# Half stage of a graph kernel: one of two tiles weighed by GpSimd, both one-hot tiles made by VectorE

## The chip, the cores and the metric

One Trainium2 chip, one core of it. Times are device microseconds of one execution of the whole program, and the number compared is the median of several executions. A core has TensorE (PE in the profile, with PEld for its weight loads), VectorE (DVE), ScalarE (ACT), GpSimd (POOL) and SyncE (SP), each with an instruction stream of its own, tied together by semaphores.

## The reference: what is computed

A graph network of two layers with residuals and layer norms, on 6250 nodes with 64 features and 206,250 directed edges. This case is about the first layer, an attention layer with 4 heads of 64 features:

```python
out_i = softplus(concat([x[i], edge_attr]) @ W).reshape(-1, 4, 64)
out_j = softplus(concat([x[j], edge_attr]) @ W).reshape(-1, 4, 64)
alpha = softplus((concat([out_i, out_j], -1) * att).sum(-1))
# batch norm over the edges, softplus, softmax over the edges of node i
out   = segment_sum(out_j * alpha[:, :, None], i).mean(1) + bias
```

The inner sum over 128 features (64 of out_i and 64 of out_j, times att, for each of the 4 heads) is what the change moves between engines. A second layer, two graph convolutions, follows.

## The kernel before, in words

Edges are sorted into tiles of 128, one edge to a partition, so that all edges of a tile have their node i in one block of 128 nodes. Two tiles make a unit (UT = 2), six units a round (BU = 6). Earlier stages (`key_stage`, `table_stage`, `spread_stage`) write to memory, for each edge, a row with softplus(out_j) (256 numbers), the edge's 64 features and its node's place in the block. `half_stage` (L1464) computes the other half, out_i, and the sum with att. It has 912 units in 152 rounds; loops hold two rounds each (`paired_parts`), so a loop's end comes once in twelve units. `before(i, j, depth, width)` names the unit that lies `depth` back, `seg` the unit that lies ahead.

Each engine has its order written out by hand. For unit j:

- SP loads the unit's rows into one of six buffers `bufh` (L1516), as soon as the sums of the unit six before have been taken (`sp_read`).
- `places` on DVE makes the one-hot tile of the unit's first tile (L1546), three units ahead. POOL makes that of the second tile (L1528), keeps the places in `nloA` (L1530) and copies the 64 edge features of both tiles to `eaC` (L1534), as soon as the rows are in.
- `turn` on PE transposes the two one-hot tiles (L1623) and eaC (L1626), one unit ahead, in front of `product`: edge features times W (L1634) and one-hot tile times the node table in three parts (L1639), all into `pre`. `body` on PE calls `turn` of unit j+1 and then `product` of unit j.
- ACT copies what was turned to `eaTh` and `oneT` (L1587, L1588) two units ahead, and for the next unit takes Exp of `pre` (L1595) and Ln of that plus one (L1599) into the second half of `bufh`. The semaphore of that Ln is `sp_ready`.
- `finish` on DVE waits for `sp_ready`, and takes for each of the two tiles and each of the four heads one multiply-and-sum over 2 x 64 elements, `bufh` times `attb` (L1559: eight instructions, two SBUF inputs each, with one small read of the accumulator behind each). Once a round the sums are copied to `alpha` (L1572).

Other stages that the text draws on: `spread_stage` before it (DVE reduces 128x400 at L933), and `message_stage` after it (L2144), where POOL multiplies the units 1 and 4 of each round by their weights (L2203, 128x512), DVE the other four (L2248, the same shape) and adds PE's result, which lies in PSUM, to `acc` (L2257).

Of the kernel before, what the change touches and what calls it, by code (L numbers as in the profile page):

```python
# [15 lines left out]
fp32 = mybir.dt.float32  # L16
bf16 = mybir.dt.bfloat16
# [5 lines left out]
P = 128  # L23
D = 64
# [1439 lines left out]
def half_stage(nc, z, m, sb, ps, sem, att):  # L1464
# [3 lines left out]
    with ExitStack() as ctx:  # L1468
# [7 lines left out]
        attb = sb(ctx, "attb", [P, 2, H, D], fp32)  # L1476
        junk = [sb(ctx, f"junk{q}", [P, UT * H, 2, D], bf16) for q in range(2)]
        sums = sb(ctx, "sums", [P, BU * UT * H], fp32)
# [5 lines left out]
        def sems(name, n=BU):  # L1484
            return [sem(ctx, f"{name}{j}") for j in range(n)]

        row_in, ea_kept, one_ready, second_ready, x_turned, o_turned, x_evac, o_evac, pre_ready, exp_done, sp_ready, \
            sp_read = (sems(s) for s in (
                "row_in", "ea_kept", "one_ready", "second_ready", "x_turned", "o_turned", "x_evac", "o_evac",
                "pre_ready", "exp_done", "sp_ready", "sp_read"))  # L1490
# [29 lines left out]
        @block.gpsimd  # L1520
        def _(eng):
            def body(i, h):
                for j in range(BU):
                    o, c = before(i, j, PRE, BU)
                    eng.wait_ge(row_in[j], (i + 1) * 16)
                    wait(eng, o_turned[o], c)
                    eng.sem_inc(keeping, 1)
                    eng.tensor_scalar(one[j % PRE][:, 1, :], m["io128b"][:, :], buf[j][:, 1, 0, C + D:C + D + 1], 0.0,  # L1528
                                      ALU.add, ALU.is_equal).then_inc(second_ready[j], 1)
                    eng.tensor_copy(m["nloA"][:, span((i * BU + j) * UT, UT)], buf[j][:, :, 0, C + D])  # L1530
                    o, c = before(i, j, 2, BU)
                    wait(eng, x_turned[o], c)
                    eng.sem_inc(keeping, 1)
                    eng.tensor_copy(eaC[j % 2][:, :, :], buf[j][:, :, 0, C:C + D]).then_inc(ea_kept[j], 1)  # L1534

            paired_parts(eng, z.its, body)

        @block.vector
        def _(eng):
            def places(i, j):  # L1540

                q = j % PRE
                o, c = before(i, j, PRE, BU)
                eng.wait_ge(row_in[j], (i + 1) * 16)
                wait(eng, o_turned[o], c)
                eng.tensor_scalar(one[q][:, 0, :], m["io128b"][:, :], buf[j][:, 0, 0, C + D:C + D + 1], 0.0,  # L1546
                                  ALU.add, ALU.is_equal).then_inc(one_ready[j], 1)

            def finish(i, j):
                q = j % 2  # L1550
                o, c = before(i, j, 2, BU)
                eng.wait_ge(sp_ready[j], i + 1)
                wait(eng, sp_read[o], c)
                if j == 0:
                    wait(eng, kept, i)
                for k in range(UT):
                    for h in range(H):
                        n = (j * UT + k) * H + h
                        ins = eng.tensor_tensor_reduce(junk[q][:, k * H + h, :, :],  # L1559
                                                       buf[j][:, k, :, h * D:(h + 1) * D],  # L1560
                                                       attb[:, :, h, :], 1.0, 0.0, ALU.mult, ALU.add,
                                                       sums[:, n:n + 1])
                ins.then_inc(sp_read[j], 1)

# [50 lines left out]
        def _(eng):  # L1615
            def turn(i, j):
                q = j % 2
                o, c = before(i, j, 2, BU)
                eng.wait_ge(one_ready[j], i + 1)
                eng.wait_ge(second_ready[j], i + 1)  # L1620
                wait(eng, o_evac[o], c)
# [1048 lines left out]
```

## Time and profile before

| | |
|---|---|
| time, median of 3 executions | 7230.75 us (7227.9 to 7233.67) |
| span of the profiled execution, first to last instruction | 6311.7 us |
| profiled execution's own total | not given; the median lies 919 us above the span |
| busy over the span: PE, DVE, ACT, POOL | 76%, 78%, 62%, 63% |
| half stage | 2526 to 4470 us |

Times in the rows are microseconds from the start of the span, unless marked ns. Register, branch, semaphore and DMA-issuing instructions don't count as busy. In a timeline a row is start, duration, engine, line, operation, output <- input, shape, count, and in brackets the idle time of the engine before it with what ended it. DVE's and ACT's instructions overlap a little, so what one costs its engine is the distance of two starts. The multiply-and-sum is called CUSTOM_DVE_ANT_1 in the profile. A span on POOL is rough.

### The profile page before, as it was taken

To read this page: it belongs to the slowest core of one execution; us is meant where nothing else is said; L and a number is where in the kernel's file an instruction comes from. 1 tells how busy PE (TensorE), PEld (TensorE's weight loads), DVE (VectorE), ACT (ScalarE), POOL (GpSimd) and SP (SyncE) were. 2 spreads that over 40 slices of the span, in tenths; PEclk is the share of its full clock that TensorE was granted. 3 is DMA by queue.
4 is the path that set the end of the run, shared out by engine and by line. 5 is a ranking of instruction groups with operands and counts; after the bars stand their busy time and mean duration, and the time that the engine had idled before them with its cause. 6 is when DMAs were issued, how large, how long until landed. Compare 5 with 4: busy or idle time off the path is not lost. (4 is left out here: it accounts for less than half of the span.)

```text
span 6311.7 us, 164797 instructions
## 1 busy us (share of the span) xinstructions
PE 4769.4 (76%) x33037; PEld 3113.2 (49%) x33038; DVE 4917.3 (78%) x25722; ACT 3904.0 (62%) x10209; POOL 3956.6 (63%) x5713
## 2 busy tenths in 40 slices
PE   1367777777777773888888888888388888875976
PEld 0234444444444442444444444444155555555976
DVE  6579888888888882999999999999777777774122
ACT  3057666666666663788888888888666666660000
POOL 1357777777777775666666666666299998870000
PEclk8589999999999997999999999999699999996978
DMA  8856666666666665555555555555277777764766
GB/s 236 261 193 228 224 222 222 213 225 222 223 213 223 222 224 198 157 155 155 155 156 155 156 155 156 155 155 155 54 219 221 221 222 218 217 190 184 317 276 234
DMA packets 905821, 1259.83 MB, mean 200 GB/s; under 512 B 267668, under 2 KB 774531, under 8 KB 884180
## 3 DMA queue, kind: packets, MB, share of 16 engines
q1 hardware_dynamic: 783812, 843.53, 47.3%
q0 software_dynamic: 88656, 333.99, 13.8%
q10 hardware_dynamic: 33216, 80.75, 3.5%
q8 instruction: 54, 0.88, 0.1%
q14 instruction: 83, 0.68, 0.0%
HBM read 832.07 MB, written 425.87 MB: 199 GB/s over the span
## 5 line engine op out<-in xcount | busy, mean ns | idle before, releaser
L872 POOL DMA_INDIRECT rows<-rowS,idx x1616 | 1628.5, 1008 | 521.3 <-issue 485.5
L1559 DVE CUSTOM_DVE_ANT_1 junk<-bufh,attb 128x128 bf16<-128x128 f32 x7296 | 1738.1, 298 | 7.0 <-ACT bufh L1599 5.5
L1528 POOL TENSOR_SCALAR one<-io128b,bufh 128x128 bf16<-128x128 bf16 x912 | 811.1, 889 | 723.1 <-DMA bufh<-rows 723.0
L2282 PE MATMUL psm<-msg,onem 128*128 128x260 f32 x3648 | 926.9, 396 | 177.7 <-issue 157.5
L1128 PE MATMUL psa<-one_c,one_s 128*128 128x392 bf16 x2352 | 560.2, 350 | 483.4 <-ACT cnts L1014 442.0
L2282 PEld LDWEIGHTS psm<-msg,onem 128*128 128x128 f32 x3648 | 644.3, 190 | 459.9 <-issue 388.9
L955 DVE TENSOR_SCALAR one_c<-ioc,code 128x392 bf16<-128x392 f16 x2352 | 790.4, 336 | 13.8
L1639 PE MATMUL pre<-P3h,oneT 128*128 x5472 | 756.5, 274 | 0.0
L1595 ACT ACTIVATE lg<-pre 128x512 f32<-128x512 f32 x912 | 544.6, 597 | 309.1 <-PE pre L1639 303.4
L2248 DVE TENSOR_TENSOR msg<-oj,alpha 128x512 f32<-128x512 f32 x608 | 494.0, 813 | 220.2 <-issue 196.2
L2218 ACT ACTIVATE dist_m<-io,nloA 128x128 f32<-128x128 f32 x1216 | 454.9, 398 | 335.3 <-PE psm L2282 325.3
L1634 PE MATMUL pre<-W2d,eaTh 64*128 64x256 f32 x3648 | 641.6, 429 | 0.0
L1639 PEld LDWEIGHTS pre<-P3h,oneT 128*128 128x128 bf16 x5472 | 460.5, 98 | 344.7 <-issue 302.4
L2207 POOL TENSOR_SCALAR onem<-io,lanes 128x128 f32<-128x128 f32 x608 | 601.7, 993 | 29.3 <-POOL heads L2194 29.3
L1021 ACT ACTIVATE lgS<-preS 128x1024 f32<-128x1024 f32 x404 | 412.5, 1021 | 329.1 <-PE preS L1117 323.6
L956 DVE TENSOR_SCALAR one_s<-io128b,pairS 128x128 bf16<-128x128 bf16 x2352 | 595.4, 253 | 0.0
L1599 ACT ACTIVATE bufh<-lg 128x512 f32<-128x512 f32 x912 | 575.9, 632 | 29.0
L1559 DVE DVE_READ_ACCUMULATOR2_ANT sums<- 128x1 f32 x7296 | 559.0, 77 | 0.1
L1111 PE MATMUL preS<-W2d,eaT 64*128 64x256 f32 x3232 | 528.4, 451 | 3.1 <-ACT eaT L1032 2.9
L1128 PEld LDWEIGHTS psa<-one_c,one_s 128*128 128x128 bf16 x2352 | 202.1, 101 | 653.0 <-issue 340.5
L1623 PE MATMUL turned<-identb,one 128*128 128x128 bf16 x1824 | 256.9, 222 | 264.2 <-DVE one L1546 170.7
L1014 ACT ACTIVATE cnts<-psa 128x392 bf16<-128x392 f32 x784 | 361.1, 486 | 137.3 <-PE psa L1128 134.9
(275 smaller groups left out, 8757.5 us busy)
## 6 DMA issues: line engine op xcount, KB each, us to landing
bufh<-rows SPq DMA_DIRECT2D x912, 322.0 KB, 3.0
oj<-rows SPq DMA_DIRECT2D x912, 256.0 KB, 2.9
adj<-adj SPq DMA_DIRECT2D x98, 1568.0 KB, 8.2
adj<-cnts ACTq DMA_DIRECT2D x49, 1568.0 KB
eaS<-in_edge_attr_dram SPq DMA_DIRECT2D x201, 256.0 KB
low<-dlow SPq DMA_DIRECT2D x202, 252.0 KB
rows<-blanktail POOLq DMA_DIRECT2D x20, 1610.0 KB
rows<-fill POOLq DMA_DIRECT2D x100, 322.0 KB
```

The costliest lines, as they stand in the source:

```text
L872: eng.indirect_dma_start(out=m["rows"][h], out_offset=bass.IndirectOffsetOnAxis(ap=idx[s][:, k:k + 1], axis=0), in_=rows[s][:, k, :], in_o ...
L955: eng.tensor_scalar(one_c[r][:, k, :], m["ioc"][:, :], code[r][:, k:k + 1], None, ALU.is_equal)
L956: ins = eng.tensor_scalar(one_s[r][:, k, :], m["io128b"][:, :], pair[q][:, k, 0:1], 0.0, ALU.add, ALU.is_equal)
L1128: mm = eng.matmul(psa[r][:, 0:z.GC], one_s[r][:, k, :], one_c[r][:, k, :], start=(k == 0), stop=(k == GT - 1))
L1528: eng.tensor_scalar(one[j % PRE][:, 1, :], m["io128b"][:, :], buf[j][:, 1, 0, C + D:C + D + 1], 0.0, ALU.add, ALU.is_equal).then_inc(secon ...
L1559: ins = eng.tensor_tensor_reduce(junk[q][:, k * H + h, :, :], buf[j][:, k, :, h * D:(h + 1) * D], attb[:, :, h, :], 1.0, 0.0, ALU.mult, AL ...
L1595: eng.activation(lg[q][:, :, :], pre[q][:, :, 0:C], ACT.Exp, accum_out=m["exps"][:, span(2 * z.NG + i * BU + j, 1)]).then_inc(exp_done[j], 1)
L1599: eng.activation(buf[j][:, :, 1, 0:C], lg[q][:, :, :], ACT.Ln, bias=1.0).then_inc(sp_ready[j], 1)
L1634: eng.matmul(pre[j % PRE][:, k, 0:C], eaT[q][k * D:(k + 1) * D, :], m["W2d"][k * D:(k + 1) * D, :], start=True, stop=False, skip_group_che ...
L1639: mm = eng.matmul(pre[j % PRE][:, k, 0:C], oneT[q][:, k * P:(k + 1) * P], P3[:, bass.ds(b, 1), n, :].rearrange("p o c -> p (o c)"), start= ...
L2207: eng.tensor_scalar(one[j][:, 1, :], m["io128"][:, :], lanes[:, j * UT + 1:j * UT + 2], 0.0, ALU.add, ALU.is_equal).then_inc(second_ready[ ...
L2282: mm = eng.matmul(psm[j][:, 0:C + H], one[q][:, k, :], msg[q][:, k, :], start=(k == 0), stop=(k == UT - 1))
```

## The change

POOL no longer makes the second one-hot tile; DVE makes both, in `places`. POOL multiplies the second tile of each unit (both halves, 512 numbers) by att into a new tile `prod`, of which there are two, when the unit's Ln is there; DVE keeps the four multiply-and-sums of the first tile and sums `prod` by one reduction. On POOL the copies are made two units ahead of the product. PE has one wait less.

```diff
-        junk = [sb(ctx, f"junk{q}", [P, UT * H, 2, D], bf16) for q in range(2)]
+        junk = [sb(ctx, f"junk{q}", [P, H, 2, D], bf16) for q in range(2)]
+        prod = [sb(ctx, f"prodh{q}", [P, 2, H, D], fp32) for q in range(2)]
...
         @block.gpsimd
         def _(eng):
+            def keep(i, j):
+                eng.wait_ge(row_in[j], (i + 1) * 16)
+                eng.sem_inc(keeping, 1)
+                eng.tensor_copy(m["nloA"][:, span((i * BU + j) * UT, UT)], buf[j][:, :, 0, C + D])
+                o, c = before(i, j, 2, BU)
+                wait(eng, x_turned[o], c)
+                eng.sem_inc(keeping, 1)
+                eng.tensor_copy(eaC[j % 2][:, :, :], buf[j][:, :, 0, C:C + D]).then_inc(ea_kept[j], 1)
+
+            def weigh(i, j):
+                o, c = before(i, j, 2, BU)
+                eng.wait_ge(sp_ready[j], i + 1)
+                wait(eng, sp_read[o], c)
+                eng.sem_inc(keeping, 1)
+                eng.tensor_tensor(prod[j % 2][:, :, :, :], buf[j][:, 1, :, 0:C].rearrange("p s (h d) -> p s h d", h=H),
+                                  attb[:, :, :, :], ALU.mult).then_inc(weighed[j], 1)
+
             def body(i, h):
                 for j in range(BU):
-                    o, c = before(i, j, PRE, BU)
-                    eng.wait_ge(row_in[j], (i + 1) * 16)
-                    wait(eng, o_turned[o], c)
-                    eng.sem_inc(keeping, 1)
-                    eng.tensor_scalar(one[j % PRE][:, 1, :], m["io128b"][:, :], buf[j][:, 1, 0, C + D:C + D + 1], 0.0,
-                                      ALU.add, ALU.is_equal).then_inc(second_ready[j], 1)
-                    eng.tensor_copy(m["nloA"][:, span((i * BU + j) * UT, UT)], buf[j][:, :, 0, C + D])
-                    o, c = before(i, j, 2, BU)
-                    wait(eng, x_turned[o], c)
-                    eng.sem_inc(keeping, 1)
-                    eng.tensor_copy(eaC[j % 2][:, :, :], buf[j][:, :, 0, C:C + D]).then_inc(ea_kept[j], 1)
-
+                    if not (last(i) and j + 2 >= BU):
+                        keep(*seg(i, j + 2, BU))
+                    weigh(i, j)
+
+            eng.wait_ge(att_in, 32)
+            keep(0, 0)
+            keep(0, 1)
             paired_parts(eng, z.its, body)
...
-                eng.tensor_scalar(one[q][:, 0, :], m["io128b"][:, :], buf[j][:, 0, 0, C + D:C + D + 1], 0.0,
-                                  ALU.add, ALU.is_equal).then_inc(one_ready[j], 1)
+                for k in range(UT):
+                    ins = eng.tensor_scalar(one[q][:, k, :], m["io128b"][:, :], buf[j][:, k, 0, C + D:C + D + 1], 0.0,
+                                            ALU.add, ALU.is_equal)
+                ins.then_inc(one_ready[j], 1)
...
-                for k in range(UT):
-                    for h in range(H):
-                        n = (j * UT + k) * H + h
-                        ins = eng.tensor_tensor_reduce(junk[q][:, k * H + h, :, :],
-                                                       buf[j][:, k, :, h * D:(h + 1) * D],
-                                                       attb[:, :, h, :], 1.0, 0.0, ALU.mult, ALU.add,
-                                                       sums[:, n:n + 1])
-                ins.then_inc(sp_read[j], 1)
+                n = j * UT * H
+                for h in range(H):
+                    eng.tensor_tensor_reduce(junk[q][:, h, :, :], buf[j][:, 0, :, h * D:(h + 1) * D],
+                                             attb[:, :, h, :], 1.0, 0.0, ALU.mult, ALU.add, sums[:, n + h:n + h + 1])
+                eng.wait_ge(weighed[j], i + 1)
+                eng.tensor_reduce(sums[:, n + H:n + 2 * H], prod[q][:, :, :, :].rearrange("p s h d -> p h s d"), AX.XY,
+                                  ALU.add).then_inc(sp_read[j], 1)
...
                 eng.wait_ge(one_ready[j], i + 1)
-                eng.wait_ge(second_ready[j], i + 1)
                 wait(eng, o_evac[o], c)
```

## Rows read from the trace of the kernel before

**Rows 1.** Busy time by stretch: a part of the spread stage, the half stage.

```profile
600.00:1000.00 400.00, 305.33 (x2319) 191.00 (x2318) 342.98 (x1541) 267.60 (x458) 307.34 (x305) 0.92 0.65 219
...
2526.00:4470.00 1944.00, 1696.60 (x11856) 961.27 (x11856) 1887.01 (x15656) 1598.93 (x4560) 1252.54 (x2736) 1.00 0.58 155
```

Columns: stretch, its length, busy time and count of PE, PEld, DVE, ACT, POOL, granted clock, DMA's share, GB/s.

**Rows 2.** Groups of instructions, whole span: busy us, mean ns, idle before.

```profile
L1559 DVE CUSTOM_DVE_ANT_1 junk<-bufh,attb 128x128 bf16<-128x128 f32 x7296 | 1738.1, 298 | 7.0 <-ACT bufh L1599 5.5
L1528 POOL TENSOR_SCALAR one<-io128b,bufh 128x128 bf16<-128x128 bf16 x912 | 811.1, 889 | 723.1 <-DMA bufh<-rows 723.0
```

**Rows 3.** Timeline of DVE in the half stage, from 3202.9 us.

```profile
3202.91 0.32 DVE L1546 TENSOR_SCALAR one<-io128b,bufh 128x128 bf16<-128x128 bf16 x1
3203.07 0.28 DVE L1559 CUSTOM_DVE_ANT_1 junk<-bufh,attb 128x128 bf16<-128x128 f32 x1
...
3203.28 0.28 DVE L1559 CUSTOM_DVE_ANT_1 junk<-bufh,attb 128x128 bf16<-128x128 f32 x1
...
3203.49 0.36 DVE L1559 CUSTOM_DVE_ANT_1 junk<-bufh,attb 128x128 bf16<-128x128 f32 x1
```

**Rows 4.** Waits from 3000 to 3500 us: in total, times, longest.

```profile
POOL one L1528 <- DMA bufh<-rows: 176.9, 235, 1.7
PEld turned L1623 <- DVE one L1546: 94.4, 181, 1.3
```

**Rows 5.** Groups of instructions on DVE: the reduction in the spread stage.

```profile
L933 DVE TENSOR_REDUCE posf<-ranks 128x8 f32<-128x400 f32 x202 | 112.8, 558 | 0.2
```

**Rows 6.** Timeline of DVE at a loop's end, from 3196.2 us.

```profile
3196.29 0.24 DVE L1572 COPY alpha<-sums 128x48 f32 x1
3196.88 0.25 DVE L1546 TENSOR_SCALAR one<-io128b,bufh 128x128 bf16<-128x128 bf16 x1 [0.35 <-issue]
```

**Rows 7.** Timeline of POOL and DVE in the message stage, 4909 to 4912.5 us.

```profile
4909.08 1.06 POOL L2203 TENSOR_TENSOR msg<-oj,heads 128x512 f32<-128x512 f32 x1
4909.43 1.25 DVE L2248 TENSOR_TENSOR msg<-oj,alpha 128x512 f32<-128x512 f32 x1 [0.51 <-issue]
4910.11 2.09 POOL L2207 TENSOR_SCALAR onem<-io,lanes 128x128 f32<-128x128 f32 x2
...
4910.95 0.68 DVE L2248 TENSOR_TENSOR msg<-oj,alpha 128x512 f32<-128x512 f32 x1
...
4912.17 0.43 DVE L2257 TENSOR_TENSOR acc<-acc,psm 128x260 f32 x1 [0.21 <-PE psm L2282]
4912.23 1.06 POOL L2203 TENSOR_TENSOR msg<-oj,heads 128x512 f32<-128x512 f32 x1
```

**Rows 8.** Timeline of POOL, PE and ACT in the half stage, 3203 to 3207 us.

```profile
3203.13 0.26 POOL L1530 COPY nloA<-bufh 128x2 f32 x1
...
3203.34 0.38 POOL L1534 COPY eaC<-bufh 128x128 f32<-128x128 f32 x1
...
3203.76 0.33 PE L1626 MATMUL turned<-ident,eaC 128*128 128x128 f32 x1 [0.19 <-POOL eaC L1534]
...
3204.66 0.83 PE L1639 MATMUL pre<-P3h,oneT 128*128 x6
...
3205.61 0.60 ACT L1595 ACTIVATE lg<-pre 128x512 f32<-128x512 f32 x1 [0.64 <-PE pre L1639]
...
3206.33 0.63 ACT L1599 ACTIVATE bufh<-lg 128x512 f32<-128x512 f32 x1
```

**Rows 9.** Timeline of POOL at the half stage's start.

```profile
2527.37 0.18 POOL L1530 COPY nloA<-bufh 128x2 f32<-128x2 f32 x1
2527.49 0.28 POOL L1534 COPY eaC<-bufh 128x128 f32<-128x128 f32 x1
```

**Rows 10.** Timeline of DVE and ACT: one unit's one-hot tile and the Ln behind it.

```profile
3200.96 0.24 DVE L1546 TENSOR_SCALAR one<-io128b,bufh 128x128 bf16<-128x128 bf16 x1
...
3203.91 0.63 ACT L1599 ACTIVATE bufh<-lg 128x512 f32<-128x512 f32 x1
```

**Rows 11.** DMA issues on the page: KB each, median us from issue to landing.

```profile
bufh<-rows SPq DMA_DIRECT2D x912, 322.0 KB, 3.0
```

More of the change, by code:

```diff
@@ L1485, in sems @@
             return [sem(ctx, f"{name}{j}") for j in range(n)]
-        row_in, ea_kept, one_ready, second_ready, x_turned, o_turned, x_evac, o_evac, pre_ready, exp_done, sp_ready, \
+        row_in, ea_kept, one_ready, weighed, x_turned, o_turned, x_evac, o_evac, pre_ready, exp_done, sp_ready, \
             sp_read = (sems(s) for s in (
-                "row_in", "ea_kept", "one_ready", "second_ready", "x_turned", "o_turned", "x_evac", "o_evac",
+                "row_in", "ea_kept", "one_ready", "weighed", "x_turned", "o_turned", "x_evac", "o_evac",
                 "pre_ready", "exp_done", "sp_ready", "sp_read"))
```

## The prediction, made before the changed kernel was built or run

> **What bounds the kernel now.** I read the busy time by stretch first. The half stage is the stretch from 2526 to 4470 us, 1944 us for 912 units of two tiles, so 2.13 us a unit; VectorE is busy for 1887 of them, PE for 1697, ScalarE for 1599, POOL for 1253, and PE's granted clock is 1.00, its upper level of 2.4 GHz [rows 1]. The groups of instructions tell what VectorE does: eight multiply-and-sum instructions of line 1559 a unit, one one-hot tile of line 1546, while POOL makes the other (line 1528) [rows 2, 3]. The timeline gives their true cost, which is the distance of two starts: 0.21 us from 3203.07 to 3203.28, and 0.16 us for a one-hot tile, 3202.91 to 3203.07 [rows 3]. The waits say that the others run behind VectorE or the row loads: in 500 us POOL waits 176.9 us for rows, PE's weight loads 94.4 us for VectorE's one-hot tile [rows 4]. Nothing holds VectorE up but its own queue. It is the bound of the stage, and a unit is 8 x 0.21 + 0.16, two instructions stretched by 0.08 each (3203.49 takes 0.36 where 3203.28 takes 0.28), and loop and copy costs.
>
> **The change, part by part, on VectorE.** Removed: four of eight multiply-and-sums, 4 x 0.21 = 0.85 us. Added: a second one-hot tile, 0.16 to 0.17, and one reduction of 512 fp32 elements to 4. The nearest row is a reduction of 400 elements in 0.558 us [rows 5]. Were all of that fixed, 512 would cost 0.56, were all of it per element, 0.558 x 512/400 = 0.71; I take 0.67, near the second, which is 0.60 start to start (instructions of 0.28 start 0.21 apart, so 0.07 overlap [rows 3]). An upper bound is 1.2, if the permuted view halved the rate; the ring below would cover that too, as VectorE has some 0.5 us to spare in it. VectorE's own work per unit becomes 0.33 + 0.85 + 0.60 + 0.04 (the copy of the sums, 0.24 once in six [rows 6]) = 1.82, and with two stretches of 0.08 by POOL's copies 1.98 us. Against 2.13 that alone would be a gain of 0.13 us a unit after loop costs.
>
> **On POOL.** Removed: its one-hot tile, 0.889 us [rows 2]. Added: a product of 512 fp32 elements with two inputs. The same shape runs on POOL in the message stage: 1.06 us, 1.03 to the next start, 4909.08 to 4910.11 [rows 7]. There one input is a broadcast, here it is a plain tile; I take 1.03, between 0.95 and 1.2. POOL's busy time, some 1.6 us a unit, is no bound. Two things about the product are.
>
> **First: the ring that it closes.** The new order on POOL is keep(0), keep(1), and then keep(j+2), weigh(j) for each unit. keep makes eaC, from which PE's line 1626 turns the tile; weigh(j) waits for sp_ready(j), ScalarE's Ln. Before, POOL waited for nothing that late. Now keep(j+1) stands behind weigh(j-2) in POOL's queue; PE turns unit j+1 ahead of the product of unit j (lines 1644 to 1649: turn, then product), so product(j) waits for keep(j+1); Exp and Ln of j follow, and weigh(j) waits for that Ln. This is a ring that goes round once in two units: weigh(j-2), keep(j+1), turn(j+1), product(j), Exp(j), Ln(j), weigh(j). Its price, from one pass of the profile [rows 8]: keep, from the start of the copy nloA at 3203.13 to the end of eaC at 3203.34 + 0.38 = 3203.72: 0.59. From there to the end of Ln, 3206.33 + 0.63 = 3206.96: 3.24 (turn at 3203.76, P3 products 3204.66 to 3205.49, Exp at 3205.61). Ln's end to POOL's start: 0.05, as from eaC's end to PE's turn in the same rows, 0.04. The product: 1.03. Sum 4.91 us in two units, **2.46 us a unit**. With keep as it runs undisturbed, 0.12 + 0.28 = 0.40 [rows 9], the sum is 4.72, or 2.36; with a product of 1.2 it is 5.1, or 2.55. I take 2.46, since POOL's copies stand beside VectorE's two-input work as they do now. Every part of the ring is a duration that a row shows, and the order is written out in the code; so the ring is the step of which I am surest.
>
> **Second: the port.** The message stage shows what POOL's product does to VectorE. VectorE's product of line 2248 takes 0.68 us alone, at 4910.95; the one that starts at 4909.43, inside POOL's product of 4909.08 to 4910.14, takes 1.25. It ended at 4910.68, so in effect it began 0.68 earlier, at 4910.00, 0.14 us before POOL's ended. VectorE's add of line 2257, which reads PSUM as one of its inputs, takes 0.43 from 4912.17 with POOL's product beside it from 4912.23: not held [rows 7]. So a VectorE instruction with two SBUF inputs stands still for the first 0.90 us of a POOL product of 1.06. The multiply-and-sums have two SBUF inputs; the one-hot tile is stretched in the half stage by POOL's work too, 0.32 at 3202.91 where 3200.96 took 0.24 [rows 3, 10], so I count it as held. The reduction has one input and nothing in PSUM; I take it as free, from the add.
>
> The Trainium skill, in SBUF — State Buffer, section SBUF: two separate sides, has this as a lock on a shared pair of ports, held "for the full instruction". For the product the trace nearly agrees (0.90 of 1.06). For POOL's copies it doesn't: eaC takes 0.38 us and costs the multiply-and-sum beside it 0.08 [rows 3, 8]. By the rule the held work would add up to 0.33 + 0.85 + 1.06 + 0.26 + 0.38 = 2.88 us a unit, by the row to 0.33 + 0.85 + 0.90 + 0.17 = 2.25, which is below the ring.
>
> Where does the 0.90 fall? If POOL's product(j+1) starts while VectorE reduces unit j, then part of it hides behind the reduction. Take a pitch of 2.46 and time 0 at the end of POOL's product(j): VectorE is freed at -0.15, makes its one-hot tiles until 0.2, the four sums until about 1.15, reduces until 1.8. POOL's next product starts at 2.46 - 1.06 = 1.40, inside the reduction, and holds VectorE until 2.31. So VectorE stands 0.5 us, its unit is 1.98 + 0.5 = 2.48, and it doesn't wait for weighed at all. That agrees with the ring, and its one-hot tiles are early enough: from their end to Ln's end are 3.34 us (3201.20 to 3204.54 [rows 10]), so the product of two units later may start at 0.2 + 3.4 = 3.6, and the ring asks it for 3.86. Both fit.
>
> **Edits at nothing.** PE's dropped wait is one of two for the same tile. The tiles of prod are used by turns, and POOL's wait for sp_read two units back is over (reduction ends at 1.8, product(j+2) starts at 3.86). Row loads are freed at the reduction's end, and three units, 7.4 us, lie before keep needs the row; the load takes 3.0 [rows 11]. POOL's new wait for att is in front of rows that land later on the same queue. Loop ends cost 0.35 us once in twelve units [rows 6], 0.03 a unit.
>
> **Sum.** 912 x (2.46 + 0.03) = 2271, and 10 for filling and draining (before: 7 to the first sum): 2281 against 1944, +337 us. The other stages are untouched. The profiled execution has a span of 6311.7; its own total isn't shown, and the median of the runs lies 919 above the span. I add the difference to the median: 7230.75 + 337 = **7568 us**. The ring's bounds, 2.36 and 2.55, give 7477 and 7650.
>
> **Rivals.**
> - *Product over the sums.* If POOL's product comes while VectorE still does its multiply-and-sums, nothing hides it: 1.98 + 0.90 + 0.03 = 2.91 us a unit, 2654 + 10, +720: 7951 us. It sustains itself: one-hot tiles end, 3.40 later POOL's product starts, and at a pitch of 2.88 that is 0.52 into the next unit's four sums, of which the last starts at 0.64. For it: at the start VectorE's sums and POOL's product of a unit wait for the same Ln. Against: the margin is 0.12 us, and once it slips past the last sum the shorter pitch holds. By the full rule of the page the pitch would be 2.88 too. Chance 0.22; with turns between both, times between 7568 and 7951, 0.13.
> - *The clock falls.* PE gets more gaps. In the spread stage, with PE busy for 305 of 400 us, the granted clock is 0.92, which is 16% of the time at 1.2 GHz [rows 1]; in the half stage it would be busy for 1.86 of 2.46 us, the same share. PE's part of the ring is 1.73 us; a sixth of it again is 0.28 in two units, 0.14 x 912 = +128: 7696 us. Against: the clock is 1.00 now, with PE idle for an eighth of the stage. Chance 0.10.
> - *Faster.* POOL's product doesn't set the pace, VectorE does: 2.01 x 912 + 10 = 1843, -101: 7130 us. It needs a ring under 4.02 us, or 4.2 to break even, so a POOL product under some 0.3 us, or a ring that is not closed, and a port that doesn't hold the sums. The rows speak against each. Chance 0.04. That the new instructions don't appear as written, with no measurable difference: 0.02.
> - The ring as forecast: 0.49.
>
> **Numbers.** Predicted 7568. The range takes the ring's low bound, the clock, and the uncovered product: 7470 to 7955, leaving out under 0.2. The runs of before spread by 0.08%, so 0.2%, 14 us, is about the least that can be told from nothing. Faster by more: 0.05; within: 0.02; slower: 0.93.
>
> **What would show it.** Right: in the half stage VectorE's sums or one-hot tiles of over 1 us once a unit, beginning inside a POOL product; PE's line 1626 waiting for POOL's eaC in nearly every unit; eaC beginning right behind a POOL product; 2.4 to 2.6 us from one POOL product to the next. A reduction near 0.67. The first rival shows POOL's product starting between two sums and a pitch of 2.9. Wrong: PE waiting for one-hot tiles and not for eaC, VectorE busy with short instructions for over nine tenths, or a POOL product far from 1.06.

## The result, and the profile after

| | median | runs | lowest to highest |
|---|---|---|---|
| before | 7230.67 us | 4 | 7227.9 to 7233.67 |
| after | 7598.36 us | 4 | 7580.75 to 7606.47 |

The ratio is 1.0508, with a 95% interval of 1.0493 to 1.0523: 367.7 us slower, where 337 were forecast. One thing has to be cleared first. The profile shown of before has a span of 6311.7 us, 919 less than its runs, and that of after 7578.9, 2 less than its run. The kernel before was therefore profiled again (run before_again below). The missing time lies in the spread stage, whose code the change leaves alone: 2094 us in the first profile, 3014 in the second and in that of after. It goes with the chip: the kernel before takes 7227 us on the one on which keep3, early and keep3_early ran, and 6315 or 6317 on the two others. All comparisons below are with runs of the kernel before on the same chip, and differences are what carries over; the half stage itself is the same in both, 1943 and 1950 us.

The busy time by stretch, of the changed kernel's half stage and of 500 us in its middle; the columns are those of [rows 1]:

```profile
3426.00:5733.00 2307.00, 1695.57 (x11856) 960.67 (x11856) 2280.82 (x10183) 1652.02 (x4560) 1421.30 (x2736) 1.00 0.48 130
4300.00:4800.00 500.00, 368.81 (x2584) 208.96 (x2585) 495.69 (x2221) 359.61 (x995) 308.36 (x595) 1.00 0.49 131
```

2307 us for 912 units are 2.53 a unit, against 2.13 [rows 1]; the stage grew by 357 us against before_again and by 364 against the first profile, of 368. VectorE is "busy" in 496 of 500 us, with 36 fewer instructions per round than before. PE's granted clock stays at 1.00.

The groups of instructions of the same kernel, from the page (busy us, mean ns, idle before), answer to [rows 2] and [rows 5]:

```profile
L1537 POOL TENSOR_TENSOR prodh<-bufh,attb 128x512 f32<-128x512 f32 x912 | 1087.8, 1193 | 882.9 <-ACT bufh L1613 882.9
...
L1573 DVE CUSTOM_DVE_ANT_1 junk<-bufh,attb 128x128 bf16<-128x128 f32 x3648 | 916.0, 302 | 3.5 <-ACT bufh L1613 3.5
...
L1560 DVE TENSOR_SCALAR one<-io128b,bufh 128x128 bf16<-128x128 bf16 x1824 | 809.9, 484 | 59.2 <-DMA bufh<-rows 59.2
...
L1576 DVE TENSOR_REDUCE sums<-prodh 128x4 f32<-128x512 f32 x912 | 615.8, 675 | 0.0
```

The reduction came out at 0.675 us, as forecast. POOL's product takes 1.18 to 1.19 instead of 1.06. The line to look at is the one-hot tile's: a mean of 484 ns, where the median of the same line is 249 and the longest 1221. That is not work but standing. One more line stands, the copy of the sums to `alpha`, once in six units:

```profile
L1586 DVE COPY alpha<-sums x152: 201/984/990, 3447.0 to 5733.5; 128x48 f32 x142, 128x48 f32<-128x48 f32 x10
```

(Shortest, median and longest in ns.) Its median is 984 ns, where it took 0.24 us in [rows 6]. The timeline shows both, of VectorE, POOL, PE and ScalarE together, from one product of POOL to the next but one:

```profile
4402.39 1.18 POOL L1537 TENSOR_TENSOR prodh<-bufh,attb 128x512 f32<-128x512 f32 x1 [1.28 <-ACT bufh L1613]
...
4402.64 0.98 DVE L1586 COPY alpha<-sums 128x48 f32 x1
...
4403.54 0.44 DVE L1560 TENSOR_SCALAR one<-io128b,bufh 128x128 bf16<-128x128 bf16 x2
4403.63 0.31 POOL L1530 COPY eaC<-bufh 128x128 f32<-128x128 f32 x1
...
4404.04 0.29 PE L1636 MATMUL turned<-identb,one 128*128 128x128 bf16 x2 [1.16 <-DVE one L1560]
...
4405.01 0.83 PE L1652 MATMUL pre<-P3h,oneT 128*128 x6
...
4405.97 0.60 ACT L1609 ACTIVATE lg<-pre 128x512 f32<-128x512 f32 x1 [0.88 <-PE pre L1652]
...
4406.69 0.63 ACT L1613 ACTIVATE bufh<-lg 128x512 f32<-128x512 f32 x1
...
4407.52 1.17 POOL L1537 TENSOR_TENSOR prodh<-bufh,attb 128x512 f32<-128x512 f32 x1 [1.30 <-ACT bufh L1613]
4407.53 1.22 DVE L1560 TENSOR_SCALAR one<-io128b,bufh 128x128 bf16<-128x128 bf16 x1
```

From product to product but one are 5.13 us, two units. At 4407.53 a one-hot tile starts beside a product and takes 1.22 us; at 4402.64 it is the copy of the sums that starts beside one, and takes 0.98. And there is the first surprise: PE waits for one-hot tiles (line 1560), in this pass 1.16 us. The waits from 4300 to 4800 us say the same of 199 units; a wait for eaC isn't among them, though this view lists only waits of 0.15 us and more:

```profile
POOL prodh L1537 <- ACT bufh L1613: 190.4, 198, 1.4
PEld turned L1636 <- DVE one L1560: 186.7, 199, 1.4
PE turned L1636 <- DVE one L1560: 131.4, 199, 1.2
```

So two theories of the pitch stood at this point. **Queue**: keep(j+1) behind weigh(j-2) in POOL's queue closes the ring, as the prediction had it; eaC ends at 4403.94, 0.2 us before its turn, and at 4406.22 only 0.06 before, so it could well be the bound by a hair. **Port**: POOL's product holds VectorE's one-hot tiles, PE waits for these, and ring and hold are one thing. A unit without the copy of the sums shows how close the two are:

```profile
4404.65 1.21 POOL L1537 TENSOR_TENSOR prodh<-bufh,attb 128x512 f32<-128x512 f32 x1 [0.71 <-ACT bufh L1613]
...
4405.35 0.72 DVE L1560 TENSOR_SCALAR one<-io128b,bufh 128x128 bf16<-128x128 bf16 x2
...
4405.93 0.29 POOL L1530 COPY eaC<-bufh 128x128 f32<-128x128 f32 x1
...
4406.13 0.29 PE L1636 MATMUL turned<-identb,one 128*128 128x128 bf16 x2 [0.29 <-DVE one L1560]
4406.28 0.33 PE L1639 MATMUL turned<-ident,eaC 128*128 128x128 f32 x1
...
4408.86 0.63 ACT L1613 ACTIVATE bufh<-lg 128x512 f32<-128x512 f32 x1
...
4409.69 1.19 POOL L1537 TENSOR_TENSOR prodh<-bufh,attb 128x512 f32<-128x512 f32 x1 [0.63 <-ACT bufh L1613]
```

PE starts on the one-hot tiles 0.06 us after they are done (4406.07) and turns eaC 0.15 behind that, 0.06 after eaC is done (4406.22). Where eaC is early, the two starts lie 0.12 apart (4404.04 and 4404.16). So here eaC comes last, by 0.02 to 0.03 us, and that is so in five of six units of the trace; in the sixth, behind the copy of the sums, it is the one-hot tiles.

### The profile page after: what moved, and what is told of

It reads as the page before. It is cut to its first block and busy times, and to the rows that moved or that the text cites. A ratio compares the mean times of both kernels' runs of the same rounds, so it can differ in the third digit from the quotient of the medians.

```text
span 7578.9 us, 160271 instructions
## 1 busy us (share of the span) xinstructions
PE 5063.1 (67%) x33037; PEld 3242.9 (43%) x33038; DVE 5287.6 (70%) x20250; ACT 3967.1 (52%) x10209; POOL 4124.8 (54%) x5713
## 5 line engine op out<-in xcount | busy, mean ns | idle before, releaser
L1537 POOL TENSOR_TENSOR prodh<-bufh,attb 128x512 f32<-128x512 f32 x912 | 1087.8, 1193 | 882.9 <-ACT bufh L1613 882.9
L1128 PE MATMUL psa<-one_c,one_s 128*128 128x392 bf16 x2352 | 627.1, 387 | 838.6 <-DVE one_s L956 591.5
L1573 DVE CUSTOM_DVE_ANT_1 junk<-bufh,attb 128x128 bf16<-128x128 f32 x3648 | 916.0, 302 | 3.5 <-ACT bufh L1613 3.5
L1560 DVE TENSOR_SCALAR one<-io128b,bufh 128x128 bf16<-128x128 bf16 x1824 | 809.9, 484 | 59.2 <-DMA bufh<-rows 59.2
L1128 PEld LDWEIGHTS psa<-one_c,one_s 128*128 128x128 bf16 x2352 | 217.8, 109 | 1039.2 <-DVE one_s L956 652.4
L2220 POOL TENSOR_SCALAR onem<-io,lanes 128x128 f32<-128x128 f32 x608 | 617.1, 1022 | 29.3 <-POOL heads L2207 29.3
L1111 PE MATMUL preS<-W2d,eaT 64*128 64x256 f32 x3232 | 611.9, 504 | 12.3 <-issue 7.2
L1576 DVE TENSOR_REDUCE sums<-prodh 128x4 f32<-128x512 f32 x912 | 615.8, 675 | 0.0
L924 DVE TENSOR_TENSOR ranks<-psr,base 128x400 f32<-128x400 f32 x202 | 115.7, 573 | 692.0 <-remote 381.2
```

Source lines behind the costliest of these rows:

```text
L1111: eng.matmul(pre[h][:, q, a * C:(a + 1) * C], eaT[j][q * D:(q + 1) * D, 2 * h + a, :], m["W2d"][q * D:(q + 1) * D, :], start=(a == 0), sto ...
L1128: mm = eng.matmul(psa[r][:, 0:z.GC], one_s[r][:, k, :], one_c[r][:, k, :], start=(k == 0), stop=(k == GT - 1))
L1537: eng.tensor_tensor(prod[j % 2][:, :, :, :], buf[j][:, 1, :, 0:C].rearrange("p s (h d) -> p s h d", h=H), attb[:, :, :, :], ALU.mult).then ...
L1560: ins = eng.tensor_scalar(one[q][:, k, :], m["io128b"][:, :], buf[j][:, k, 0, C + D:C + D + 1], 0.0, ALU.add, ALU.is_equal)
L1573: eng.tensor_tensor_reduce(junk[q][:, h, :, :], buf[j][:, 0, :, h * D:(h + 1) * D], attb[:, :, h, :], 1.0, 0.0, ALU.mult, ALU.add, sums[:, ...
L1576: eng.tensor_reduce(sums[:, n + H:n + 2 * H], prod[q][:, :, :, :].rearrange("p s h d -> p h s d"), AX.XY, ALU.add).then_inc(sp_read[j], 1)
```

## The experiments

Pitches are the length of the half stage, from its first to its last instruction on `bufh` and `sums`, by 912.

| run | against before | half stage | us a unit |
|---|---|---|---|
| before (both profiles) | | 1943, 1950 us | 2.13, 2.14 |
| after | +367.7 | 2308 | 2.53 |
| keep3 | +356.5 | 2291 | 2.51 |
| early | +653.0 | 2593 | 2.84 |
| keep3_early | +614.3 | 2564 | 2.81 |
| aligned | +217.7 | 2158 | 2.37 |
| no_product | -196.7 | 1742 | 1.91 |
| free_product | +568.3 | 2510 | 2.75 |
| onehot_only | +73.0 | 2014 | 2.21 |
| extra_product | +729.5 | 2673 | 2.93 |
| psum_extra | +12.3 | 1969 | 2.16 |
| psum_before | -109.9 | 1835 | 2.01 |
| psum_keep3_early | +240.4 | 2181 | 2.39 |

**before_again.**

> The kernel before, unchanged, for a second profile. The profile shown of it has a span of 6311.7 us and its runs take 7230.7; the changed kernel's span is 2 us under its own time. Theory: the 919 us lie in the spread stage, which took 2094 us in the profile of before and 3014 in that of after, though the change doesn't touch it, and the runs of before had the long one too: span near 7229, half stage 1944 us (2.13 us a unit). Rival: the half stage of the timed runs is itself longer than 1944, and the change's price is less or more than the 363 us that the two profiles give.

Span 7218.6 us. The busy time by stretch, of its spread stage and its half stage:

```profile
356.00:3370.00 3014.00, 1901.10 (x12214) 1136.70 (x12214) 1763.39 (x7959) 1417.32 (x2395) 1600.19 (x1605) 0.79 0.46 154
3424.00:5374.00 1950.00, 1702.71 (x11856) 964.58 (x11856) 1887.95 (x15656) 1602.26 (x4560) 1254.73 (x2736) 1.00 0.57 154
```

The theory holds: the half stage is as in [rows 1], the spread stage 920 us longer with the same instructions. The cause is open.

**keep3.** POOL's copies come three units ahead:

```diff
-        eaC = [sb(ctx, f"eaC{q}", [P, UT, D], fp32) for q in range(2)]
+        eaC = [sb(ctx, f"eaC{q}", [P, UT, D], fp32) for q in range(PRE)]
...
-                    if not (last(i) and j + 2 >= BU):
-                        keep(*seg(i, j + 2, BU))
+                    if not (last(i) and j + PRE >= BU):
+                        keep(*seg(i, j + PRE, BU))
                     weigh(i, j)
```

> The changed kernel with POOL's copies three units ahead of the product instead of two (three eaC tiles). It opens the ring through POOL's queue: keep(j+1) then stands behind weigh(j-3). Queue theory (this ring sets the 2.53 us a unit of the changed kernel): the pitch falls, to 2.25 to 2.42, total 7390 to 7500. Port theory (the one-hot tiles, held by POOL's product, set it): nothing changes within 20 us, 7580 to 7615, and PE goes on waiting for line 1560's tiles.

7583.55 us against 7227.05, ratio 1.0486 (1.0465 to 1.0507). The queue theory in its own terms falls: its ring is open, and 2.53 became 2.51 where 2.25 to 2.42 had been expected. The intervals of the two ratios overlap, so even the 0.02 can't be told from nothing. The timeline of this kernel:

```profile
4402.99 1.18 POOL L1537 TENSOR_TENSOR prodh<-bufh,attb 128x512 f32<-128x512 f32 x1 [0.80 <-ACT bufh L1614]
...
4403.08 1.30 DVE L1561 TENSOR_SCALAR one<-io128b,bufh 128x128 bf16<-128x128 bf16 x2
...
4404.44 0.28 PE L1637 MATMUL turned<-identb,one 128*128 128x128 bf16 x2 [0.96 <-DVE one L1561]
...
4407.94 1.18 POOL L1537 TENSOR_TENSOR prodh<-bufh,attb 128x512 f32<-128x512 f32 x1 [0.80 <-ACT bufh L1614]
```

The ring goes by the other link: the product of 4402.99 holds the one-hot tiles of 4403.08 for a microsecond, they are done at 4404.38, PE takes them at 4404.44, and two units later POOL starts again, 4.95 us on. Both paths close a ring of nearly the same length, and this edit opens only one.

**early.** VectorE makes the one-hot tiles between the four sums and the reduction:

```diff
                     eng.tensor_tensor_reduce(...)
+                if not (last(i) and j + PRE + 1 >= BU):
+                    places(*seg(i, j + PRE + 1, BU))
                 eng.wait_ge(weighed[j], i + 1)
                 eng.tensor_reduce(...)
...
-                    if not (last(i) and j + PRE >= BU):
-                        places(*seg(i, j + PRE, BU))
                     finish(i, j)
```

> The changed kernel with the one-hot tiles of unit j+4 made on VectorE between the four sums and the reduction of unit j, instead of those behind the reduction: they then come before POOL's next product starts. Port theory (one-hot tiles held by the product are late for PE): the pitch falls to 2.40 to 2.47, total 7480 to 7540, if nothing stands behind it; queue theory: eaC is just as late, so the pitch stays at 2.50 to 2.53, total 7570 to 7610, and PE now waits for eaC instead of one-hot tiles. A rival on the other side: POOL's product now falls on the sums, 2.9 us a unit, 7930.

7880.0 us against 7227.05, ratio 1.0911 (1.0893 to 1.0929): the rival on the other side, and neither theory's first answer. The timeline of this kernel:

```profile
4403.33 0.28 DVE L1573 CUSTOM_DVE_ANT_1 junk<-bufh,attb 128x128 bf16<-128x128 f32 x1
4403.54 0.28 DVE L1573 CUSTOM_DVE_ANT_1 junk<-bufh,attb 128x128 bf16<-128x128 f32 x1
...
4403.59 1.27 POOL L1537 TENSOR_TENSOR prodh<-bufh,attb 128x512 f32<-128x512 f32 x1 [0.98 <-DVE sums L1578]
...
4403.75 1.26 DVE L1573 CUSTOM_DVE_ANT_1 junk<-bufh,attb 128x128 bf16<-128x128 f32 x1
4404.94 0.28 DVE L1573 CUSTOM_DVE_ANT_1 junk<-bufh,attb 128x128 bf16<-128x128 f32 x1
```

POOL now waits for line 1578, the reduction that frees its tile, so the product starts right behind a reduction, in every unit, and the third sum pays for it: 1.26 us. Nothing hides it. It is the first rival of the prediction, at 2.84 a unit where 2.91 was worked out. In the changed kernel the tiles and copies that come late for PE were what delayed POOL's product until the next reduction.

**keep3_early.** Both edits.

> Both edits: copies three units ahead and one-hot tiles before the reduction. If both rings are closed at the same length (queue and port), only this one is faster: VectorE's own 1.98 us and a hold of 1.03 (product 1.18 less 0.15) of which at most 0.6 hides behind the reduction, 2.4 us a unit, total 7480. If VectorE's occupancy alone sets the pace, nothing changes, 7580 to 7610. If the product comes earlier and meets the sums: 2.9 to 3.0 a unit, 7930 to 8030.

7841.39 us against 7227.05, ratio 1.0852 (1.0831 to 1.0873), the third case of the expectation, though 2.81 and +614 lie below its 2.9 to 3.0 and +700 to +800. POOL's product itself waits for only 71 us in all, but the copy in front of it in the queue waits for rows, now three units ahead: 841 us in the 2270 from 3430 to 5700.

```profile
4406.27 0.20 POOL L1526 COPY nloA<-bufh 128x2 f32 x1 [1.11 <-DMA bufh<-rows]
...
4406.76 1.18 POOL L1537 TENSOR_TENSOR prodh<-bufh,attb 128x512 f32<-128x512 f32 x1
```

So the row loads now set when the product starts, on the median 0.6 us after what it waits for itself is there. It then holds a sum in some seven of ten units and a one-hot tile in most of the others. Removing both rings makes the kernel slower: they had put more of the product beside the reduction (0.39 us a unit in the changed kernel, 0.16 here).

**no_product.** POOL's product is left out and VectorE reduces zeros, which are written once ahead of the loop.

```diff
-                    weigh(i, j)
+                    pass
...
-                eng.wait_ge(weighed[j], i + 1)
                 eng.tensor_reduce(...)
```

> The changed kernel without POOL's product: VectorE reduces tiles of zeros that are filled once, and doesn't wait for POOL; everything else is as in the changed kernel, so the weights of every second tile are left out. It takes away the hold and the ring at once and shows VectorE's own work. Both theories: 1.85 to 2.0 us a unit, half stage 1690 to 1840, total 6980 to 7130. Rival (the reduction or the second one-hot tile, not the product, costs more than counted): over 2.2 us a unit, over 7300.

6118.6 us against 6315.27 on its chip, ratio 0.9687 (0.967 to 0.9703): -196.7 us, where -100 to -250 had been expected (the absolute numbers stand for a chip with 7230). VectorE's own work is 1.91 us a unit with its loop costs. The product on POOL costs 2.53 - 1.91 = 0.62 us a unit, 565 us; the relief that it buys is 0.22. The traces tell on what the 0.62 falls. From this kernel to the changed one, the mean of a one-hot tile goes from 256 to 484 ns (0.46 us a unit), of a sum from 284 to 302 (0.07), and of the copy of the sums from 229 to 960, once in six units (0.12).

**free_product.** POOL's product waits for no Ln and multiplies att by itself:

```diff
-                eng.wait_ge(sp_ready[j], i + 1)
                 wait(eng, sp_read[o], c)
                 eng.sem_inc(keeping, 1)
-                eng.tensor_tensor(prod[j % 2][:, :, :, :], buf[j][:, 1, :, 0:C].rearrange("p s (h d) -> p s h d", h=H),
+                eng.tensor_tensor(prod[j % 2][:, :, :, :], attb[:, :, :, :],
                                   attb[:, :, :, :], ALU.mult).then_inc(weighed[j], 1)
```

> The changed kernel with a POOL product of the same size that multiplies att by itself and waits for no Ln, only for its tile to be read: the sums of every second tile are left out. No ring goes through it any more, the port is used as before. Port theory: the product now starts as soon as the reduction two units back has freed its tile, so it falls on the one-hot tiles and sums and nothing hides it: 1.98 + 1.03 = 3.0 us a unit, total 8030, slower than the changed kernel. Queue theory: without the ring VectorE's own pace, 2.0 to 2.4, total 7120 to 7480.

6883.6 us against 6315.27, ratio 1.0903 (1.0885 to 1.0921): +568.3, slower than the changed kernel's +367.7 although nothing waits for Ln on POOL. The direction is the port theory's; the size is 2.75 instead of 3.0, because this product takes 1.04 us and not 1.18 and VectorE's own work is 1.91 and not 1.98. The timeline:

```profile
3202.76 1.04 POOL L1536 TENSOR_TENSOR prodh<-attb 128x512 f32<-128x512 f32 x1 [1.15 <-DVE sums L1575]
...
3202.83 1.13 DVE L1572 CUSTOM_DVE_ANT_1 junk<-bufh,attb 128x128 bf16<-128x128 f32 x1
3203.89 0.28 DVE L1572 CUSTOM_DVE_ANT_1 junk<-bufh,attb 128x128 bf16<-128x128 f32 x1
```

The sum takes 0.85 us more than its 0.28, and 1.91 + 0.85 = 2.76 is the pitch.

**onehot_only.** The part of the change that moves the one-hot tile, alone, on the kernel before.

> The kernel before with one part of the change: VectorE makes both one-hot tiles, POOL only copies, and all eight sums stay on VectorE. Expected by every theory: one more one-hot tile, 0.16 to 0.17, less up to 0.08 for the POOL instruction that no longer stretches one of VectorE's: 2.21 to 2.30 us a unit, total 7305 to 7385. If it costs more than that, the hold isn't the main part of the change's price.

6388.29 us against 6315.27, ratio 1.0114 (1.0097 to 1.0131): +73.0 us, 0.08 a unit, at the low end (75 had been the least): a one-hot tile more on VectorE costs 0.16, and the POOL instruction that goes no longer stretches one of its sums.

**extra_product.** The kernel before, and one product more on POOL that nobody reads:

```diff
+                    o, c = before(i, j, 2, BU)
+                    wait(eng, weighed[o], c)
+                    eng.sem_inc(keeping, 1)
+                    eng.tensor_tensor(prod[j % 2][:, :, :, :], attb[:, :, :, :], attb[:, :, :, :],
+                                      ALU.mult).then_inc(weighed[j], 1)
```

> The kernel before, complete, with one more POOL product a unit of 512 elements (att by att) into a tile that nobody reads. It prices the hold on VectorE alone. POOL's own work becomes 0.89 + 0.18 + 0.30 + 1.18 = 2.5 us a unit. Port theory: VectorE, with eight sums and one one-hot tile and no reduction to hide behind, is held for 1.03 a unit: 2.13 + 1.03 = 3.1, total 8130. Rival (no hold on the multiply-and-sums, POOL itself becomes the bound): 2.5 to 2.6 us a unit, total 7570 to 7660.

7044.77 us against 6315.27, ratio 1.1156 (1.1138 to 1.1175): +729.5, 0.80 us a unit, for work whose result goes nowhere. 8130 had been expected on a chip with 7230, that is +900. The product here takes 1.07 us (median), and VectorE doesn't stand for all of it: the instruction that is held starts 0.11 us after the product, on the median, and is let go 0.13 before its end, which leaves 0.83.

**psum_extra.** The same kernel, with att copied once into a bank of PSUM, so that the sums have one input in SBUF (`pre` gets two tiles instead of three to make room, and PE's product waits accordingly):

```diff
-        pre = [ps(ctx, f"pre{q}", [P, UT, 2 * C], fp32) for q in range(PRE)]
+        pre = [ps(ctx, f"pre{q}", [P, UT, 2 * C], fp32) for q in range(2)]
+        attp = ps(ctx, "attp", [P, 2, C], fp32)
...
-                                                       attb[:, :, h, :], 1.0, 0.0, ALU.mult, ALU.add,
+                                                       attp[:, :, h * D:(h + 1) * D], 1.0, 0.0, ALU.mult, ALU.add,
...
+            eng.tensor_copy(attp[:, :, :], attb[:, :, :, :].rearrange("p s h d -> p s (h d)")).then_inc(att_kept, 1)
+            eng.wait_ge(att_kept, 1)
```

> The kernel with the extra POOL product (2.93 us a unit, 729 us over before), and att in PSUM. The direct test of the port: the same POOL product beside the same multiply-and-sums, which now have one SBUF input. Port theory: they are not held, only the one-hot tile is; POOL's own work of 2.4 to 2.5 us then sets the pitch, 2.4 to 2.65, half stage 2190 to 2420, 250 to 480 us over before; no multiply-and-sum over 0.5 us in the trace. Rival (the hold comes from something else, as SBUF banks or POOL's writes): 2.9 as before.

6328.83 us against 6316.57, ratio 1.0018 (1.0008 to 1.0028). +729.5 us became +12.3. This is the experiment that settles the matter for the sums. The groups of instructions, first of extra_product:

```profile
L1567 DVE CUSTOM_DVE_ANT_1 junk<-bufh,attb 128x128 bf16<-128x128 f32 x7296 | 2294.2, 374 | 5.0 <-ACT bufh L1607 4.8
```

and of psum_extra:

```profile
L1569 DVE CUSTOM_DVE_ANT_1 junk<-bufh,attp 128x128 bf16<-128x128 f32 x7296 | 1585.1, 279 | 38.3 <-ACT bufh L1611 19.2 <-issue 0.5
L1556 DVE TENSOR_SCALAR one<-io128b,bufh 128x128 bf16<-128x128 bf16 x912 | 369.6, 405 | 24.4 <-issue 22.1 <-DMA bufh<-rows 1.8
```

The same 7296 sums beside the same POOL products, 374 ns on the mean with att in SBUF and 279 with att in PSUM; the longest was 1.50 us and is 0.33. The one-hot tile (both its inputs in SBUF, one of them the scalar of the partition) is still held, 405 ns on the mean and 1.68 at most. That also answers a rival which this edit alone leaves, that the sums stood because both engines read the one tile of att: the one-hot tile and the copy of the sums (0.84 us at most here, 1.05 in extra_product) don't read it and are held beside the same product. POOL's pitch came out better than expected, 2.07 us in the timeline, as its own instructions no longer wait either: the one-hot tile on POOL takes 0.73 instead of 0.88.

**psum_before.** The kernel before with att in PSUM, and for that two tiles of `pre` instead of three.

> The kernel before, with att in a bank of PSUM instead of SBUF (pre has two buffers for three, to free it). The eight multiply-and-sums have one SBUF input each. Port theory: POOL's three instructions no longer stretch them, 2 x 0.08 a unit less: 1.97 to 2.05 us a unit if an input from PSUM costs VectorE nothing, 80 to 150 us under before. Rival: an input from PSUM costs each multiply-and-sum some fixed time, 8 x 0.03 or more: 100 us or more over before. Second rival: two buffers for pre stop PE: PE would wait for Exp, line 1595.

6206.72 us against 6316.57, ratio 0.9826 (0.981 to 0.9843): **faster than the kernel before**, by 110 us, with nothing left out. The timeline of VectorE:

```profile
3202.43 0.28 DVE L1561 CUSTOM_DVE_ANT_1 junk<-bufh,attp 128x128 bf16<-128x128 f32 x1
3202.64 0.28 DVE L1561 CUSTOM_DVE_ANT_1 junk<-bufh,attp 128x128 bf16<-128x128 f32 x1
3202.84 0.28 DVE L1561 CUSTOM_DVE_ANT_1 junk<-bufh,attp 128x128 bf16<-128x128 f32 x1
```

No sum of 0.36 is left [rows 3], and the longest of all is 0.291. An input from PSUM costs nothing: 0.21 us from start to start, as before. In the stage's 1835 us PE is busy for 1682 and ScalarE for 1597, VectorE for 1746; that little more is to be had on VectorE alone is an inference from this and wasn't tested.

**psum_keep3_early.** keep3_early with att in PSUM.

> The changed kernel with copies three units ahead, one-hot tiles before the reduction, and att in PSUM. Neither ring is left and the sums aren't held; the product starts at a reduction's end and runs beside the four sums. Port theory: what stays is VectorE's own 1.85 to 1.91 us and what of the hold reaches the one-hot tiles, 0.2 to 0.3: 2.05 to 2.2 us a unit, within 80 us of the kernel before on either side, and some 300 us faster than the changed kernel. Rival (the order, not the port, makes 2.81): stays above 2.6, over 430 us above before.

6556.95 us against 6316.57, ratio 1.0381 (1.0364 to 1.0399), +240.4 where 80 at most had been expected. The sums are free (longest 0.289), the pitch is 2.39 all the same. Its timeline shows two of the costs that the expectation had left out or made too small:

```profile
3201.62 0.42 DVE L1563 TENSOR_SCALAR one<-io128b,bufh 128x128 bf16<-128x128 bf16 x2 [0.66 <-DMA bufh<-rows]
...
3206.50 1.18 POOL L1539 TENSOR_TENSOR prodh<-bufh,attb 128x512 f32<-128x512 f32 x1
...
3206.65 1.24 DVE L1563 TENSOR_SCALAR one<-io128b,bufh 128x128 bf16<-128x128 bf16 x2
```

With one-hot tiles made four units ahead VectorE waits for row loads (159 us in the stage, 4 in no_product), and the tiles themselves are still held: their mean is 359 ns where it is 256 in no_product, 188 us. The third cost is the copy of the sums, 717 ns on the mean for 229, 74 us. Together that is 417 of the 439 us that this stage is longer than that of no_product.

**aligned.** keep3_early, with POOL's product of unit j+1 also waiting for the last sum of unit j:

```diff
                 wait(eng, sp_read[o], c)
+                o, c = before(i, j, 1, BU)
+                wait(eng, summed[o], c)
                 eng.sem_inc(keeping, 1)
                 eng.tensor_tensor(prod[...]
...
+                ins.then_inc(summed[j], 1)
```

> The kernel with copies three units ahead and one-hot tiles before the reduction (2.81 us a unit), and POOL's product of unit j+1 now also waits for the last sum of unit j. So it starts when VectorE has only two one-hot tiles and the reduction before its next sums. Port theory (the hold costs only what isn't hidden behind work with one input): part of the hold of 1.03 falls on the one-hot tiles, the rest hides behind the reduction, as does POOL's start: 1.91 + 1.03 - 0.45 = 2.45 to 2.6 us a unit, half stage 2230 to 2370, 290 to 430 us over the kernel before. Rival (the pitch of 2.81 has another cause, as PE's slower clock or the later one-hot tiles): it stays at 2.8 or grows, 600 us or more over before.

6534.25 us against 6316.57, ratio 1.0342 (1.0325 to 1.036), +217.7: a wait added takes keep3_early from 2.81 to 2.37 us a unit, below the range expected. The timeline:

```profile
3204.87 0.43 DVE L1564 TENSOR_SCALAR one<-io128b,bufh 128x128 bf16<-128x128 bf16 x2
3205.22 0.67 DVE L1583 TENSOR_REDUCE sums<-prodh 128x4 f32<-128x512 f32 x1
...
3205.22 1.18 POOL L1540 TENSOR_TENSOR prodh<-bufh,attb 128x512 f32<-128x512 f32 x1
...
3205.81 0.73 DVE L1577 CUSTOM_DVE_ANT_1 junk<-bufh,attb 128x128 bf16<-128x128 f32 x1
```

Product and reduction start together, the whole reduction is cover, and only 0.45 us of the hold is left on the next sum (0.73 for 0.28): 1.91 + 0.45 = 2.36. This is the least of the orders tried with att in SBUF, and it is still slower than before.

## Why the prediction was right, and where

The time was forecast at 7568 us and is 7598; the forecast difference 337, the measured one 368.

- **VectorE's own work**, 1.98 + 0.03 a unit: 1.91 with loop costs. 0.10 too much: POOL, without its one-hot tile, stretches hardly any of it (the sums' mean in no_product is 284 ns, their median 281), where 0.16 had been put in. The reduction, 0.67, was 0.675.
- **The port.** Right in kind and the heart of the price. From one pair of rows in another stage [rows 7] came that a VectorE instruction with two SBUF inputs stands until 0.14 us before the end of a POOL product. In early the held sum ends at 4405.01, so in effect it began at 4404.73, 0.13 before the product's end at 4404.86. The Trainium skill's sentence in SBUF — State Buffer, section SBUF: two separate sides, that the one that starts first has the ports "for the whole instruction", is near that for the product; psum_extra agrees with one of its conditions, two SBUF inputs, 729 us against 12. The sentence has a second condition, a VectorE instruction in a 2-port perf mode, and no run here shows in which mode the one-hot tile or the copy ran. For POOL's short copies it is still too strong: they cost a sum 0.08 us of their 0.30 to 0.38.
- **The hidden part.** Forecast: 0.5 of 0.90 us stand, the rest is behind the reduction. Measured: 0.62 of 1.03 (1.18 less 0.15) stand. Right in kind, and aligned and early are its two ends, 0.45 and 0.93. What the forecast had left out is the copy of the sums, put at 0.04 a unit and taken as free: 0.12 of the 0.62 falls on it.
- **The ring through POOL's queue**, the step called surest, is there, 4.99 to 5.14 us for two units where 4.91 was worked out, and eaC is the last to arrive in five of six units. But its terms came out otherwise than forecast, and the total is right in part by luck. From 4404.65 to 4409.69 they are: the product 1.21 (1.03), the copies to eaC's end 0.36 (0.59), from there to Ln's end 3.27 (3.24), and from Ln's end to POOL's start 0.20 (0.05). One term was 0.23 too large and two were 0.33 too small.
- **"Its one-hot tiles are early enough"** was the part that was wrong. They were given 0.26 us to spare (3.6 against 3.86) and have 0.02 to 0.03. Their end was well forecast, 0.21 us after the product's end for 0.2; but the copies that they race take 0.36 and not 0.59. So opening the queue's ring in keep3 gives back 0.02 us a unit at most: the path over the port stands right behind it. Of the prediction's own signs, PE waiting for one-hot tiles was to mean wrong and PE waiting for eaC right, and the trace has both: the first in long waits, the second in 0.02 us behind them.
- **The product's size**, 1.03 to 1.06: 1.18 measured here and 1.04 with att for both inputs. The row of the message stage had a broadcast for one input; the tie to the operands is shown, its cause isn't.
- **Product over the sums**, the rival at 0.22: it hardly happened in the changed kernel (9 of 3648 sums stand for long) and happened at once in early, at 2.84 where 2.91 was worked out. Its margin had been put at 0.12 us.
- **The clock**, 0.10: the granted clock of the half stage stayed at 1.00.

## What to carry to other kernels

Before work goes from VectorE to POOL, count for both what each instruction reads from SBUF: here a POOL product of 1.18 us stops VectorE for up to 1.03 in the sums with two SBUF inputs, in the one-hot tiles and in the copy of the sums, so handing over 0.85 us of work cost 0.40 a unit more than it saved, and only the reduction could hide part of it. One input alone doesn't make an instruction free: the copy has one and stands, the reduction has one and doesn't. For the sums the cure is on VectorE's side: a constant operand moved from SBUF to PSUM ended their hold and made the kernel before 1.7% faster. It doesn't save this change, as tiles and copy are still held (psum_keep3_early, +240 us). And where two paths leave from one event and arrive within a few hundredths of a microsecond, a sum along either comes out right, and an edit that opens just one of them gives back next to nothing.

## What the runs showed of the hardware that was not expected

- A PSUM input costs VectorE's multiply-and-sum nothing: 0.28 us, 0.21 from start to start, with att in SBUF or in PSUM, and its mean falls from 298 ns to 280.
- Of VectorE's instructions with one input, the reduction is never held (669 to 680 ns in all 912 of after), and the copy of 48 sums is, 0.98 us for 0.20 to 0.24. The cause is open here.
- POOL's instructions gain as well. With att in PSUM its one-hot tile takes 716 ns on the mean instead of 889 [rows 2], its eaC copy 290 instead of 347.
- The spread stage takes 2094 us on one chip and 3014 on another, with the same instructions, granted clock 0.92 in [rows 1] and 0.79 in before_again. The cause is open.
- keep3_early ran from 3500 to 4000 us with a granted clock of 0.85, so part of it at 1.2 GHz, and early with 1.00, though PE worked through about as many instructions in both (2319 and 2291). Over the half stage the granted clock was 0.88 in keep3_early, 0.90 in extra_product, 0.93 in free_product and 0.98 in psum_keep3_early, and 0.99 or more in the others. VectorE was busy or standing for 97 to 98% of the stage in the first three, so little of their time is PE's. The rows of keep3_early and of early:

```profile
3500.00:4000.00 500.00, 375.89 (x2319) 209.90 (x2317) 486.13 (x1993) 318.76 (x890) 300.78 (x534) 0.85 0.44 118
...
3500.00:4000.00 500.00, 316.16 (x2291) 179.53 (x2292) 486.69 (x1966) 324.47 (x882) 311.57 (x528) 1.00 0.43 116
```
